# Graph network on one core: three edits in the edge pass, the relation sums and the last layer

## The chip, the cores and the metric

The kernel runs on one core of one Trainium2 chip. The metric is the device time of one execution in microseconds (us), median of several runs. A core has five engines with queues of their own: TensorE (PE; matrix products, its weight loads shown as PEld), VectorE (DVE), ScalarE (ACT), GpSimd (POOL), which here only gathers and scatters rows by index, and SyncE (SP), which issues plain transfers. They wait for one another through semaphores only. SBUF is the on-chip memory, PSUM the memory that TensorE writes and VectorE and ScalarE can read.

## The reference

6250 nodes with 64 features, 200,000 edges sorted by destination. Four layers, each on the layer-normed, rectified features `h`, each added to `x`:

```python
# layer 0: attention; i = src, j = dst, act = softplus
out_i = act(concat(h[i], edge_attr) @ W); out_j = act(concat(h[j], edge_attr) @ W)   # 4 heads x 64
alpha = act((concat(out_i, out_j) * att).sum(-1))            # one number per edge and head
alpha = segment_softmax(act(batch_norm(alpha)), i)
x += segment_sum(out_j * alpha, i).mean(heads) + bias
# layer 1
x += segment_sum(h[src], dst)
# layer 2, twice: h @ W[r] for 24 relations, one of them per edge
h = relu(segment_sum(hw[src, rel], dst) / deg);  x += h
# layer 3: five 64x64 products; neigh_low/high are means over the edges
low  = relu(h W_self)      + mean_agg(relu(h W_neigh) * deg**-0.5)
high = relu(h W_self_high) - mean_agg(relu(h W_neigh_high) * deg**-0.5)
ident = relu(h W_id)
a = softmax(sigmoid([low.w_low, high.w_high, ident.w_mlp]) @ W_att.T / 3)
x += 3 * (a0 * low + a1 * high + a2 * ident)
```

## The kernel before

Nodes stand in 50 blocks of 128 (49 used), edges in tiles of 128 (`P`), eight tiles (`G`) a group. The program is a chain of stages with barriers between them.

**Edge pass** (`edge_pass`, 202 groups in a loop of 101 trips, two groups a trip). It makes `out_i`, `out_j` and their products with `att` for each edge, sorts the edges by source (a counting sort) and scatters the rows to `rows_d`. For one group the queues run as follows. GpSimd gathers eight tiles of features (L785) and scatters the eight tiles of finished rows (L793) behind a wait for `rows_ready` (L791). TensorE takes the tiles in four pairs: a pair's products go to one of two PSUM tiles `z` (L873, L876) behind a wait for `z_free` (L870); between the pairs stand small products that keep a running count (L886, L890), each after a copy by ScalarE (L818, the wait is L885). At the group's end TensorE turns the next group's features (L866), ScalarE copies them (L824), and the next group's first pair needs that copy. ScalarE makes exp and ln (L828, L834) of each pair. VectorE does, pair by pair, `outs(q, p)`: two operations that finish softplus (L950 to `prod`, L954 to `rows`), a wait for both (L956), after which it gives `z` back to TensorE, two multiplications by `att` (L958, L960), a wait for both (L962) and a sum (L963). Between the pairs stand eight `ranks` (L941, each counts earlier edges of the same source within a tile), the next group's one-hots (L927 to L936), `pick` and `base` (L988, L992), `place` (L997, behind waits for the ranks), a copy of the edges' ends (L998), and at the end the heads' sum (L1001), which gives `rows_ready`. All orders are written out by hand.

**Relation sums** (`gather_sum`, two runs of 202 groups). GpSimd gathers 128 rows at a time (L1522), TensorE multiplies them with one-hots, VectorE adds the results to `acc` (L1223) and makes the next one-hots with one comparison per group (L1564), of `iota` and `dloc`, both in SBUF. GpSimd waits only for a free ring buffer and the index lists.

**Last layer.** Four stages: a norm; `channel_tables`, which per block turns `h` (L1802), multiplies it by five weights (L1812), rectifies (L1847) and scales (L1837); `dense_sum` (tag `l3s`), which multiplies the table with a 49-block matrix of edge counts, in two halves of its columns (L1437), each followed by an evacuation and transpositions (L1450 to L1469); and `channel_mix` (L1889 to L1913), VectorE on whole 3200-column tiles, then one store (L1873).

## Time and profile before

| | us |
|---|---|
| median of 3 runs | 14033.08 (14031.82 to 14033.41) |
| profiled execution | 14016.92, its span 14015.4 |
| edge pass, about 510 to 5384 | 4874 |
| softmax, attention, second layer, table, to 8690 | 3306 |
| relation sums, about 8690 to 10820 and 11098 to 13125 | 2130 and 2027 |
| last layer, 13160 to the end | 855 |
| busy in the span: PE, DVE, ACT, POOL | 7345.0, 7365.5, 3395.4, 8457.6 |

All busy shares are averages over stages in which different engines are the last. In a timeline a row gives start, duration, engine (a trailing q: the queue), line, operation, output and inputs, and in brackets the engine's idle time before it and what ended it. A group of part 5 gives busy time, mean duration, and idle time. Windows give busy us for PE, PEld, DVE, ACT and POOL in that order, then the granted share of TensorE's clock (1.00 is 2.4 GHz, 0.50 is 1.2 GHz), the DMA engines' busy share and GB/s. Durations of VectorE overlap the next start by a little, so what an operation costs is read from start to start.

### The profile page before, as it was taken

To read this page: it belongs to the slowest core of one execution; us is meant where nothing else is said; L and a number is where in the kernel's file an instruction comes from. 1 tells how busy PE (TensorE), PEld (TensorE's weight loads), DVE (VectorE), ACT (ScalarE), POOL (GpSimd) and SP (SyncE) were. 2 spreads that over 40 slices of the span, in tenths; PEclk is the share of its full clock that TensorE was granted. 3 is DMA by queue.
4 is the path that set the end of the run, shared out by engine and by line. 5 is a ranking of instruction groups with operands and counts; after the bars stand their busy time and mean duration, and the time that the engine had idled before them with its cause. 6 is when DMAs were issued, how large, how long until landed. Compare 5 with 4: busy or idle time off the path is not lost. (4 is left out here: it accounts for less than half of the span.)

```text
span 14015.4 us, 154885 instructions
## 1 busy us (share of the span) xinstructions
PE 7345.0 (52%) x27414; PEld 5002.7 (36%) x27414; DVE 7365.5 (53%) x15655; ACT 3395.4 (24%) x7069; POOL 8457.6 (60%) x8196
## 2 busy tenths in 40 slices
PE   4577767776777772035551297333333533333387
PEld 4344444444444441025551033333333333333233
DVE  6688888888888884647772002222223222222301
ACT  0244444444444442036661001000000100000100
POOL 1366666666666662877777501777776477777300
PEclk9888888888888886556665698555555655555588
DMA  1344444444444448036661285111111311111065
GB/s 23 91 140 143 141 142 144 139 145 140 143 140 142 140 142 65 10 105 181 182 182 53 85 294 190 25 26 25 26 25 24 128 26 26 26 26 26 11 243 212
DMA packets 1037353, 1462.78 MB, mean 104 GB/s; under 512 B 518414, under 2 KB 733934, under 8 KB 1011937
## 3 DMA queue, kind: packets, MB, share of 16 engines
q1 hardware_dynamic: 651986, 1075.95, 24.6%
q0 software_dynamic: 284800, 382.51, 10.2%
q10 hardware_dynamic: 100368, 2.41, 0.8%
q14 instruction: 165, 1.35, 0.0%
q8 instruction: 34, 0.56, 0.0%
HBM read 946.06 MB, written 512.36 MB: 104 GB/s over the span
## 5 line engine op out<-in xcount | busy, mean ns | idle before, releaser
L1522 POOL DMA_INDIRECT l2s_got<-rel_d,l2s_idx x3232 | 3252.5, 1006 | 1899.4 <-POOLq L1519 1006.0
L1548 PE MATMUL l2s_ps<-l2s_got,l2s_oh 128*128 128x65 f32 (+1 forms) x6464 | 1473.2, 421 | 2797.5 <-PEq L1546 2790.4
L873 PE MATMUL edge_z<-edge_w,edge_feats 128*128 128x512 f32 x3232 | 2092.0, 735 | 877.7 <-PEq L870 877.7
L1548 PEld LDWEIGHTS l2s_ps<-l2s_got,l2s_oh 128*128 128x128 f32 x6464 | 1409.0, 330 | 2863.0 <-issue 2863.0
L793 POOL DMA_INDIRECT rows_d<-edge_rows,edge_place x1624 | 1657.3, 1021 | 1100.1 <-POOLq L791 661.4
L1223 DVE TENSOR_TENSOR net_acc<-net_acc,l2s_ps 128x65 f32 (+1 forms) x3232 | 720.4, 223 | 2735.8 <-DVEq L1570 1877.4
L1241 POOL DMA_INDIRECT count_d<-all_list_val,all_list_idx x1568 | 1821.0, 1161 | 503.4 <-issue 464.2
L785 POOL DMA_INDIRECT edge_gath<-h_d,edge_idx x1624 | 1652.9, 1018 | 495.0 <-issue 494.7
L1354 PE MATMUL at_ps<-at_msg,at_oh 128*128 128x128 f32 x3520 | 746.3, 399 | 879.8 <-PEq L1350 863.3
L876 PE MATMUL edge_z<-edge_products,edge_oh_dstT 128*128 x3232 | 1155.5, 445 | 0.0
L876 PEld LDWEIGHTS edge_z<-edge_products,edge_oh_dstT 128*128 128x128 f32 x3232 | 737.4, 228 | 1010.2 <-issue 1010.2
L828 ACT ACTIVATE edge_soft<-edge_z 128x1024 f32<-128x1024 f32 x808 | 827.4, 1024 | 1068.2 <-ACTq L839 1035.1
L963 DVE TENSOR_REDUCE edge_dots<-edge_prod 128x16 f32<-128x1024 f32 x808 | 986.0, 1220 | 118.1
L873 PEld LDWEIGHTS edge_z<-edge_w,edge_feats 128*128 128x128 f32 x3232 | 661.1, 226 | 1047.4 <-issue 968.0
L1354 PEld LDWEIGHTS at_ps<-at_msg,at_oh 128*128 128x128 f32 x3520 | 693.9, 302 | 932.2 <-issue 932.2
L886 PE MATMUL edge_at<-edge_upto,edge_oh_loT 128*128 128x50 f32 x3232 | 594.8, 267 | 514.8 <-PEq L885 513.7
L834 ACT ACTIVATE edge_soft<-edge_soft 128x1024 f32<-128x1024 f32 x808 | 855.5, 1059 | 29.3
L886 PEld LDWEIGHTS edge_at<-edge_upto,edge_oh_loT 128*128 128x128 f32 x3232 | 580.1, 199 | 693.5 <-issue 635.0
L241 ACT ACT_TABLE_LOAD x4 | 5.1, 1283 | 3264.9 <-ACTq L240 3264.9
L1437 PE MATMUL l1s_ps<-l1s_cnt,l_h 128*64 128x512 f32 (+1 forms) x1274 | 519.4, 571 | 526.0 <-PEq L1435 526.0
L818 ACT COPY edge_upto<-edge_nxt 128x49 f32<-128x49 f32 x1616 | 316.4, 196 | 1441.8 <-ACTq L817 1432.9
L958 DVE TENSOR_TENSOR edge_prod<-edge_prod,edge_att 128x512 f32<-128x512 f32 x808 | 559.5, 692 | 195.3 <-DVEq L956 187.4
(364 smaller groups left out, 10171.3 us busy)
## 6 DMA issues: line engine op xcount, KB each, us to landing
at_rows<-rows_d SPq DMA_DIRECT2D x444, 528.0 KB
count_d<-edge_zero SPq DMA_DIRECT2D x202, 994.0 KB
l1s_cnt<-count_d SPq DMA_DIRECT2D x49, 1600.0 KB, 6.3
l3s_cnt<-count_d SPq DMA_DIRECT2D x49, 1600.0 KB, 6.3
rel_d<-l2t_out SPq DMA_DIRECT2D x100, 768.0 KB, 3.3
l1s_cnt<-count_d SPq DMA_DIRECT2D x49, 1536.0 KB, 6.0
l3s_cnt<-count_d SPq DMA_DIRECT2D x49, 1536.0 KB, 6.0
edge_drow<-loc_d SPq DMA_DIRECT2D x203, 256.0 KB
```

The costliest lines, as they stand in the source:

```text
L785: pool.indirect_dma_start(out=gath[q][:, j * D:(j + 1) * D], out_offset=None, in_=net.h0_d, in_offset=bass.IndirectOffsetOnAxis(ap=idx[q][ ...
L793: pool.indirect_dma_start(out=net.rows_d, out_offset=bass.IndirectOffsetOnAxis(ap=place[q][:, j:j + 1], axis=0), in_=rows[q][:, j, :], in_ ...
L828: s.activation(soft, z, ACT.Exp).then_inc(exp_made, 1)
L834: s.activation(soft, soft, ACT.Ln, bias=1.0).then_inc(ready, 1)
L873: pe.matmul(z[p % 2][:, t, :], feats[q][:, j * P:(j + 1) * P], w[:, :], start=True, stop=False, skip_group_check=True)
L876: ins = pe.matmul(z[p % 2][:, t, OUTJ:WIDE], oh_dstT[q][:, j * P:(j + 1) * P], products[:, bass.ds(blocks[j], OUTJ)], start=False, stop=Tr ...
L886: ins = pe.matmul(at_hi[:, j, :], oh_loT[q][:, j * P:(j + 1) * P], upto[j % 2][:, :], start=True, stop=True)
L963: v.tensor_reduce(dots[:, tiles, :].rearrange("p t h -> p (t h)"), prod[:, :, :].rearrange("p t (h d) -> p (t h) d", d=D), AX.X, ALU.add). ...
L1241: pool.indirect_dma_start(out=cells, out_offset=bass.IndirectOffsetOnAxis(ap=net.list_idx[i][:, k:k + 1], axis=0), in_=net.list_val[i][:, ...
L1354: ins = pe.matmul(ps[q][:, j, :], oh[q][:, n, :], msg[q][:, n, :], start=k == 0, stop=k == SPAN - 1)
L1522: pool.indirect_dma_start(out=got[r][:, j, 0:cols], out_offset=None, in_=table, in_offset=bass.IndirectOffsetOnAxis(ap=idx[i][:, k:k + 1], ...
L1548: ins = pe.matmul(ps[q][:, j, 0:wide], oh[q][:, j, :], got[r][:, j, 0:wide], start=True, stop=True)
```

## The change

Three edits.

1. Edge pass, VectorE's order. Each pair now writes `rows` first, then `prod`; one rank stands between the second of these and the multiplications, one between the multiplications and the sum, which is now a function `dot(p)` of its own. In pair 2 `pick` also stands ahead of the sum; in pair 3 the copy of the ends and `place` do.
2. Relation sums. The comparison reads `iota` from a copy in PSUM, made once a run.
3. Last layer. `channel_tables`, `dense_sum` and `channel_mix` become one stage. Two blocks of the table are made first; block b+2 is made between the matmuls of block b of the first half. The mix runs in two halves of 25 blocks, the first beside the second half's matmuls, and each half is stored by itself.

The buffers of the count lists also get a scope of their own, which only changes addresses.

```diff
-            def ranks(q, half):
...
+            def rank_of(q, j):
+                return v.scalar_tensor_tensor(
+                    junk_r[:, j, :], srow[q][:, j * P:(j + 1) * P], src_g[q][:, j:j + 1],
+                    before[:, :], ALU.is_equal, ALU.mult, accum_out=rank[:, j:j + 1])
 
             def outs(q, p, scattered_before=None):
                 v.wait_ge(soft_ready, 1).then_inc(soft_ready, -1)
+                if scattered_before is not None:
+                    v.wait_ge(scattered[q], scattered_before)
+                v.scalar_tensor_tensor(rows[q][:, tiles, 0:OUTJ], ..., ALU.min, ALU.max)
                 v.wait_ge(dotted, 1).then_inc(dotted, -1)
                 v.scalar_tensor_tensor(prod[:, :, 0:OUTJ], ..., ALU.min, ALU.max).then_inc(out_made, 1)
-                if scattered_before is not None:
-                    v.wait_ge(scattered[q], scattered_before)
-                v.scalar_tensor_tensor(rows[q][:, tiles, 0:OUTJ], ...).then_inc(out_made, 1)
-                v.wait_ge(out_made, 2).then_inc(out_made, -2)
+                rank_of(q, 2 * p)
+                v.wait_ge(out_made, 1).then_inc(out_made, -1)
                 v.sem_inc(z_free, 1)
                 v.tensor_tensor(prod[:, :, 0:OUTJ], ..., ALU.mult)
                 v.tensor_tensor(prod[:, :, OUTJ:WIDE], ..., ALU.mult).then_inc(multiplied, 1)
-                v.wait_ge(multiplied, 2).then_inc(multiplied, -2)
+                last = rank_of(q, 2 * p + 1)
+                if p == HALF - 1:
+                    last.then_inc(ranked, 1)
+            def dot(p):
+                v.wait_ge(multiplied, 1).then_inc(multiplied, -1)
                 v.tensor_reduce(dots[:, tiles, :]..., ALU.add).then_inc(dotted, 1)
...
                     outs(q, 2)
                     v.wait_ge(at_ready, 1).then_inc(at_ready, -1)
                     v.tensor_tensor(pick[:, :, :], ..., ALU.mult).then_inc(picked, 1)
+                    dot(2)
                     v.wait_ge(picked, 1).then_inc(picked, -1)
                     v.sem_inc(at_free, 1)
                     v.tensor_reduce(base[:, :], pick[:, :, :], AX.X, ALU.add).then_inc(based, 1)
-                    ranks(q, 1).then_inc(ranked, 1)
+                    outs(q, 3)
+                    v.tensor_copy(rows[q][:, :, OUTJ + HEADS:OUTJ + HEADS + 2], net.ends[:, bass.ds(w0, G), :])
+                    v.wait_ge(based, 1).then_inc(based, -1)
                     v.wait_ge(ranked, 1).then_inc(ranked, -1)
                     v.sem_inc(ids_free, 1)
-                    v.wait_ge(based, 1).then_inc(based, -1)
                     v.tensor_tensor(place[q][:, :], rank[:, :], base[:, :], ALU.add)
-                    v.tensor_copy(rows[q][:, :, OUTJ + HEADS:OUTJ + HEADS + 2], net.ends[:, bass.ds(w0, G), :])
-                    outs(q, 3)
+                    dot(3)
...
+        iota = t.ps("iota", [P, P])
...
-                    v.tensor_tensor(oh[q][:, :, :], net.iota[:, None, :].to_broadcast([P, G, P]),
+                    v.tensor_tensor(oh[q][:, :, :], iota[:, None, :].to_broadcast([P, G, P]),
...
+def channel_layer(net, norm, acc, own, table):
...
+                for b in TWO:
+                    turn_row(b)
+                    products(b)
+                for b0, b1 in halves:
...
+                    for b in range(NBU):
+                        pe.wait_ge(loaded[n % RING], 16).then_inc(loaded[n % RING], -16)
+                        for c in range(0, cols, 512):
+                            if c == 3 * 512 and b0 == 0 and b + 2 < NB:
+                                turn_row(b + 2)
+                            ins = pe.matmul(ps[:, c:min(c + 512, cols)], table[:, b, :], ...)
...
+                        if b0 == 0 and b + 2 < NB:
+                            products(b + 2)
...
+                tables()
+                v.wait_ge(mix_loaded, 64)
+                for b0, b1 in halves:
+                    sums(b0, b1)
+                    mix(b0, b1)
```

VectorE's queue before, at the start of a group of the edge pass (`edge_prod` and `edge_rows` are the softplus outputs, `edge_junk_r` marks a rank):

```order
L950 SCALAR_TENSOR_TENSOR edge_prod<-edge_soft,edge_z 128x2x256
L953 REGISTER_ALU x2
L954 SCALAR_TENSOR_TENSOR edge_rows<-edge_soft,edge_z 128x2x256
L958 TENSOR_TENSOR edge_prod<-edge_prod,edge_att 128x2x256
L960 TENSOR_TENSOR edge_prod<-edge_rows,edge_att 128x2x256
L963 TENSOR_REDUCE edge_dots<-edge_prod 128x16
L941 SCALAR_TENSOR_TENSOR edge_junk_r,edge_rank<-edge_srow,edge_src_g,edge_before 128x128 x4
```

The same place now:

```order
L948 REGISTER_ALU x2
L949 SCALAR_TENSOR_TENSOR edge_rows<-edge_soft,edge_z 128x2x256
L952 SCALAR_TENSOR_TENSOR edge_prod<-edge_soft,edge_z 128x2x256
L940 SCALAR_TENSOR_TENSOR edge_junk_r,edge_rank<-edge_srow,edge_src_g,edge_before 128x128
L957 TENSOR_TENSOR edge_prod<-edge_prod,edge_att 128x2x256
L959 TENSOR_TENSOR edge_prod<-edge_rows,edge_att 128x2x256
L940 SCALAR_TENSOR_TENSOR edge_junk_r,edge_rank<-edge_srow,edge_src_g,edge_before 128x128
L968 TENSOR_REDUCE edge_dots<-edge_prod 128x16
```

The ranks, four in a row before, stand singly ahead of the multiplications and of the sum; the register instructions for the scatter's wait stand ahead of the first output.

TensorE's queue before, at the end of the tables and the start of the count sum (`ch_tp` holds a turned block, `l3s_ps` the sum):

```order
L1802 MATMUL ch_tp<-all_ident,ch_hs 65x128
L1812 MATMUL ch_ps<-ch_ws,ch_ht 128x320
L118 REGISTER_ALU
L118 COMPARE_AND_BRANCH
L1789 UNCONDITIONAL_BRANCH
L1429 UNCONDITIONAL_BRANCH
L1437 MATMUL l3s_ps<-l3s_cnt,l3t_table 128x512 x6
L1437 MATMUL l3s_ps<-l3s_cnt,l3t_table 128x128
```

The same work now:

```order
L1855 MATMUL ch_tp<-ch_ws,ch_ht 128x320
L1870 MATMUL ch_ps<-ch_cnt,net_table 128x512 x3
L1851 MATMUL ch_tp<-all_ident,net_h 64x128
L1870 MATMUL ch_ps<-ch_cnt,net_table 128x512 x3
L1870 MATMUL ch_ps<-ch_cnt,net_table 128x128
L1855 MATMUL ch_tp<-ch_ws,ch_ht 128x320
```

Between the seven count matmuls of a block now stands the transposition, and behind them the product, of a later block; the two branches, which mark a change of stage, are gone.

## Rows read from the trace of the kernel before

**Rows 1.** Windows of two stretches: length, busy us (x instructions), PEclk, DMA share.
```profile
510.00:5384.00 4874.00, 3471.70 (x12120) 2113.13 (x12120) 4312.15 (x9292) 2273.34 (x4341) 3286.75 (x3224) 0.87 0.47 141
...
13160.00:13374.00 214.00, 78.46 (x151) 32.90 (x151) 48.65 (x202) 48.58 (x75) 0.00 (x0) 0.50 0.00 0
```

**Rows 2.** Source view of line 1001: ns min/median/max, first and last start.
```profile
L1001 DVE TENSOR_TENSOR edge_rows<-edge_dots x202: 191/192/196, 542.5 to 5383.8; 128x32 f32<-128x32 f32 x101
```

**Rows 3.** VectorE's timeline in one group: start us, duration, engine, line, idle time.
```profile
3010.59 0.68 DVE L950 SCALAR_TENSOR_TENSOR edge_prod<-edge_soft,edge_z 128x512 f32<-128x512 f32 x1
...
3012.11 0.69 DVE L958 TENSOR_TENSOR edge_prod<-edge_prod,edge_att 128x512 f32<-128x512 f32 x1 [0.24 <-DVEq L956]
3012.72 0.69 DVE L960 TENSOR_TENSOR edge_prod<-edge_rows,edge_att 128x512 f32<-128x512 f32 x1
3013.55 1.22 DVE L963 TENSOR_REDUCE edge_dots<-edge_prod 128x16 f32<-128x1024 f32 x1
3014.69 0.84 DVE L988 TENSOR_TENSOR edge_pick<-edge_oh_hi,edge_at 128x400 f32<-128x400 bf16 x1
3015.77 0.57 DVE L992 TENSOR_REDUCE edge_base<-edge_pick 128x8 f32<-128x400 f32 x1 [0.24 <-DVEq L990]
...
3016.80 0.35 DVE L941 SCALAR_TENSOR_TENSOR edge_junk_r<-edge_srow,edge_src_g,edge_before 128x128 bf16<-128x128 int16 x1
...
3017.07 0.35 DVE L941 SCALAR_TENSOR_TENSOR edge_junk_r<-edge_srow,edge_src_g,edge_before 128x128 bf16<-128x128 int16 x1
...
3017.78 0.17 DVE L997 TENSOR_TENSOR edge_place<-edge_rank,edge_base 128x8 uint32<-128x8 f32 x1 [0.35 <-DVEq L996]
...
3018.30 0.69 DVE L950 SCALAR_TENSOR_TENSOR edge_prod<-edge_soft,edge_z 128x512 f32<-128x512 f32 x1
```

**Rows 4.** TensorE's timeline there: the first matmul of each pair of tiles.
```profile
3005.80 1.10 PE L873 MATMUL edge_z<-edge_w,edge_feats 128*128 128x512 f32 x2 [0.18 <-PEq L870]
...
3012.93 1.10 PE L873 MATMUL edge_z<-edge_w,edge_feats 128*128 128x512 f32 x2 [2.68 <-PEq L870]
...
3019.88 1.10 PE L873 MATMUL edge_z<-edge_w,edge_feats 128*128 128x512 f32 x2 [0.81 <-PEq L870]
...
3026.42 1.06 PE L873 MATMUL edge_z<-edge_w,edge_feats 128*128 128x512 f32 x2
```

**Rows 5.** Short windows in the same group of tiles; columns as in rows 1.
```profile
3010.70:3014.10 3.40, 1.17 (x4) 0.70 (x5) 3.01 (x5) 3.23 (x5) 2.79 (x3) 1.00 0.12 31
3014.10:3017.60 3.50, 3.46 (x9) 1.98 (x7) 3.09 (x11) 1.44 (x3) 2.58 (x4) 0.51 0.12 26
```

**Rows 6.** Timeline of GpSimd: the first scatter of a group.
```profile
3023.64 0.99 POOL L793 DMA_INDIRECT rows_d<-edge_rows,edge_place  x1 [3.17 <-POOLq L791]
```

**Rows 7.** Page, part 5, relation gathers: busy us, mean ns, idle before.
```profile
L1522 POOL DMA_INDIRECT l2s_got<-rel_d,l2s_idx x3232 | 3252.5, 1006 | 1899.4 <-POOLq L1519 1006.0
```

**Rows 8.** Timeline of a relation sum: gathers beside an addition and beside a one-hot.
```profile
10005.55 0.95 POOL L1522 DMA_INDIRECT l2s_got<-rel_d,l2s_idx  x1 [0.30 <-issue]
10005.72 0.23 DVE L1223 TENSOR_TENSOR net_acc<-net_acc,l2s_ps 128x65 f32 x1 [0.30 <-DVEq L1224]
...
10008.84 1.23 DVE L1564 TENSOR_TENSOR l2s_oh<-all_iota,all_dloc 128x1024 f32<-128x1024 f32 x1 [0.81 <-DVEq L1584]
10009.32 1.57 POOL L1522 DMA_INDIRECT l2s_got<-rel_d,l2s_idx  x1 [0.30 <-issue]
```

**Rows 9.** Timeline of the last layer, as before.
```profile
13380.94 11.34 PE L1437 MATMUL l3s_ps<-l3s_cnt,l3t_table 128*128 128x512 f32 x24 [8.52 <-PEq L1435]
...
13646.05 3.49 DVE L1460 COPY l3s_turn<-l3s_ps 128x3200 f32<-128x3200 f32 x1 [272.21 <-DVEq L1459]
...
13917.92 3.36 DVE L1460 COPY l3s_turn<-l3s_ps 128x3072 f32<-128x3072 f32 x1 [254.95 <-DVEq L1459]
...
13939.25 3.49 DVE L1889 TENSOR_TENSOR mix_tmp<-net_acc,net_rdeg 128x3200 f32<-128x3200 f32 x1 [5.84 <-DMA mix_w<-in_W_att]
...
14006.13 0.40 SPq L1873 DMA_DIRECT2D out<-net_x  x1
```

More of the change, by code:

```diff
@@ L1774, in _ @@
                 done(v.tensor_tensor(net.x[:, :, :], net.x[:, :, :], h[:, 0:NB, :], ALU.add))
[L1777 removed]
+def channel_layer(net, norm, acc, own, table):
     nc, a = net.nc, net.a
+    RING = 3
+    halves = ((0, 25), (25, NB))
+    used = lambda b1: min(b1, NBU)
+    most = 25 * P
+    wide = 2 * D
     with Mem(nc, "ch") as t:
         ws = t.sb("ws", [D + 1, 5 * D])
[L1781 to L1782 removed]
         ht = [t.sb(f"ht{q}", [D + 1, P]) for q in TWO]
[L1784 to L1788 removed]
+        cnt = [t.sb(f"cnt{r}", [P, most]) for r in range(RING)]
+        wa = t.sb("wa", [P, 3, D])
+        w3 = t.sb("w3", [P, 3, 3])
+        lg = t.sb("lg", [P, 25, 3])
+        at = t.sb("at", [P, 25, 3])
+        pr = t.sb("pr", [P, 25, 3])
+        mx = t.sb("mx", [P, 25])
+        turn = norm.sq[:, :, :].rearrange("p b d -> p (b d)")
+        tmp = norm.blocks[:, 0:25, :]
+        ps = t.ps("ps", [P, most])
+        tp = t.ps("tp", [P, 512])
+        product, row = tp[:, 0:5 * D], tp[0:D, 512 - P:512]
+        some = 512 // wide
+        target = by_block(acc)
+        count_rows = net.count_d[0:NU * LD].rearrange("(b p c) -> b p c", p=P, c=LD)
+        sem = lambda name: net.sem("ch_" + name)
+        loaded = [sem(f"loaded{r}") for r in range(RING)]
+        cnt_free, summed, moved, turned, taken = (sem(x) for x in ("cnt_free", "summed", "moved", "turned", "taken"))
+        weights_loaded, mix_loaded, row_turned, copied, done, kept, scaled = (
+            sem(x) for x in ("weights_loaded", "mix_loaded", "row_turned", "copied", "done", "kept", "scaled"))
+        logits, squashed, shifted, raised = (sem(x) for x in ("logits", "squashed", "shifted", "raised"))
+        mixed, stored = sem("mixed"), sem("stored")
         with nc.Block() as block:
@@ L1805, in _, with turn_row @@
-                pe.wait_ge(weights_loaded, 160)
-                turn(0)
-                with Loop(nc, pe, NB // 2):
-                    for q in TWO:
-                        pe.wait_ge(copied, 1).then_inc(copied, -1)
-                        turn(1 - q)
-                        pe.wait_ge(scaled, 1).then_inc(scaled, -1)
-                        pe.matmul(ps[q][:, :], ht[q][:, :], ws[:, :], start=True, stop=True).then_inc(done, 1)
+                def turn_row(b):
+                    if b:
+                        pe.wait_ge(scaled, 1).then_inc(scaled, -1)
+                    pe.transpose(row, norm.blocks[:, b, :], net.ident[:, :]).then_inc(row_turned, 1)
@@ new lines, in products @@
+                def products(b):
+                    pe.wait_ge(copied, 1).then_inc(copied, -1)
+                    pe.matmul(product, ht[b % 2][:, :], ws[:, :], start=True, stop=True).then_inc(done, 1)
+                pe.wait_ge(weights_loaded, 160)
+                for b in TWO:
+                    turn_row(b)
+                    products(b)
+                n = 0
+                for b0, b1 in halves:
+                    blocks = used(b1) - b0
+                    cols = blocks * P
+                    for b in range(NBU):
+                        pe.wait_ge(loaded[n % RING], 16).then_inc(loaded[n % RING], -16)
+                        for c in range(0, cols, 512):
+                            if c == 3 * 512 and b0 == 0 and b + 2 < NB:
+                                turn_row(b + 2)
+                            ins = pe.matmul(ps[:, c:min(c + 512, cols)], table[:, b, :],
+                                            cnt[n % RING][:, c:min(c + 512, cols)], start=b == 0, stop=b == NBU - 1)
+                        if b < NBU - 1:
+                            ins.then_inc(cnt_free, 1)
+                        else:
+                            ins.then_inc(summed, 1)
+                        if b0 == 0 and b + 2 < NB:
+                            products(b + 2)
+                        n += 1
+                    if b0 == 0:
+                        pe.wait_ge(scaled, 1).then_inc(scaled, -1)
+                    pe.wait_ge(moved, 1).then_inc(moved, -1)
+                    pe.sem_inc(cnt_free, 1)
+                    for i, k0 in enumerate(range(0, blocks, some)):
+                        if i:
+                            pe.wait_ge(taken, 1).then_inc(taken, -1)
+                        for k in range(k0, min(k0 + some, blocks)):
+                            ins = pe.transpose(tp[:, (k - k0) * wide:(k - k0 + 1) * wide],
+                                               turn[:, k * P:(k + 1) * P], net.ident[:, :])
+                        ins.then_inc(turned, 1)
+                    pe.wait_ge(taken, 1).then_inc(taken, -1)
@@ new lines, in _ @@
+            @block.scalar
+            def _(s):
+                for b in range(NB):
+                    s.wait_ge(done, 1).then_inc(done, -1)
+                    s.activation(own[:, b, :], product[:, 0:3 * D], ACT.Relu).then_inc(kept, 1)
+                for _ in halves:
+                    s.wait_ge(logits, 1).then_inc(logits, -1)
+                    s.activation(lg[:, :, :], lg[:, :, :], ACT.Sigmoid).then_inc(squashed, 1)
+                    s.wait_ge(shifted, 1).then_inc(shifted, -1)
+                    s.activation(at[:, :, :], at[:, :, :], ACT.Exp).then_inc(raised, 1)
@@ new lines, in sums @@
+                def sums(b0, b1):
+                    blocks = used(b1) - b0
+                    cols = blocks * P
+                    v.wait_ge(summed, 1).then_inc(summed, -1)
+                    v.tensor_copy(turn[:, 0:cols], ps[:, 0:cols]).then_inc(moved, 1)
+                    for k0 in range(0, blocks, some):
+                        k1 = min(k0 + some, blocks)
+                        v.wait_ge(turned, 1).then_inc(turned, -1)
+                        got = tp[:, 0:(k1 - k0) * wide].rearrange("p (k w) -> p k w", w=wide)
+                        own_done(v.tensor_copy(target[:, b0 + k0:b0 + k1, 0:wide], got))
+                        v.sem_inc(taken, 1)
```

189 lines of the change are left out of this document (71 added, 118 removed).

## The prediction, made before the change was run

> **What bounds the kernel now.** I read the windows first, since the stages have different limits. The edge pass is 4874 us of the 14015, with VectorE busy 88% of it (4312 us) and TensorE's granted clock at 0.87 [rows 1]. Line 1001 comes once a group, from 542.5 to 5383.8 in 202 rows, so a group takes 4841.3/201 = 24.09 us [rows 2]. The reader should then look at VectorE's timeline in one group [rows 3]: the only idle it shows stands behind its own semaphores (0.24, 0.24, 0.35 us), never behind ScalarE or TensorE. So VectorE's own program is the group. TensorE waits 2.68 and 0.81 us ahead of pairs [rows 4], GpSimd 3.17 us for finished rows [rows 6]. In the relation sums the idle in front of a gather is 0.30 us, its pitch from issue [rows 8], with VectorE's additions far apart: GpSimd is the bound there. In the last layer the stages follow one another with nothing beside them [rows 1, 9].
>
> **The change, edge pass.** All pitches are from start to start [rows 3]. Multiplication to multiplication is 0.61, rank to rank 0.27.
>
> (a) Two outputs and their wait take 12.11 - 10.59 = 1.52; with 0.61 for the first, the second output to the multiplication is 0.91. A rank put there would let the multiplication start at 0.61 + 0.27 = 0.88, inside the wait. The rank is free: 4 x 0.27 = 1.08 us a group.
> (b) Second multiplication to sum is 0.83. With a rank it is 0.61 + 0.27 = 0.88, so 0.83 + 0.27 - 0.88 = 0.22, four times 0.88 us.
> (c) `pick` to `base` is 1.08 with its 0.24 of waiting. Behind `pick` now comes the sum, at about 0.84 - 0.08 = 0.76, and `base` follows the sum at the usual 1.14: 0.32 us.
> (d) Last rank to `place` is 0.71, with 0.35 idle. The copy of the ends now lies in it. `place` and that copy take 0.52 together, so its half, 0.26, goes; one wait is also satisfied earlier. Bounds 0.26 and 0.45; I take 0.35.
> (e) The register instructions for the scatter's wait stand ahead of the first output, behind the short L1001. No row prices them. Bounds 0 (hidden) and +0.35 (the longest idle that short instructions leave); I take +0.12.
>
> Sum: 1.08 + 0.88 + 0.32 + 0.35 - 0.12 = 2.5, so VectorE alone would do a group in 21.6 us.
>
> Then the next engines are late. GpSimd's group is the period less its wait beyond the usual 0.30: 24.09 - 2.87 = 21.2, some tenths more when its gathers no longer rest beside pair 3. TensorE: from the third pair in [rows 4] (pair 3 at 3005.80) to the next group's first 7.13; to its second 6.95, less 0.81 of waiting for VectorE, 6.14; to its third 6.54; the rest of the period 24.09 - 20.62 = 3.47, less 0.18, 3.29. Together 23.1 us as clocked here, more than 21.6. But a granted share of 0.87 means that 2 x 0.13 = 0.26 of the period, 6.3 us, ran at 1.2 instead of 2.4 GHz; at the upper level throughout the cycle would be about 23.1 - 3.1 = 20.0. The clock fell to 0.51 behind a stretch in which TensorE was busy 1.17 of 3.4 us, the wait before the next group's first pair, and that stretch ran at 1.00 [rows 5]. That wait mostly stays (it hangs on ScalarE's copy of the features, not on VectorE); the 0.81 goes. So I expect the second low stretch of a group to come less often, not always to vanish. VectorE's pace leaves TensorE 1.6 us of low-clock loss, half of today's.
>
> Three engines with 21.6, 21.2 to 21.6 and 20.0 to 23.1 do not give 21.6. I add 0.4: 22.0 us, a gain of 2.09 x 202 = 422 us. Bounds: 21.5 (-523) and 23.0 (-220).
>
> The added order of waits costs nothing else as I read it. The scatter's wait now holds back both outputs and so `z_free`, but the eight scatters it asks for start right behind their group's rows [rows 6] and last 8 x 21.2/16 = 10.6, with a full period to go. `ids_free` comes after pair 3, some 3 us later than before; SyncE's row loads that it releases are needed two pairs into the next group but one use later, over 7 us on. `at_free` comes behind `pick` and the sum's issue, still before TensorE has finished the next first pair.
>
> **Relation sums.** A gather beside an addition (SBUF and PSUM in) takes 0.95 us; one that overlaps the one-hot (both inputs in SBUF, 1.23 us) takes 1.57 [rows 8]. The mean of all 3232 is 1.006 [rows 7], so the stretching is 3232 x (1.006 - 0.950) = 181 us, all on GpSimd's chain, which is the bound. With `iota` in PSUM the one-hot has one SBUF input, like the addition. I take all 181; bounds 0 and 181. VectorE may take longer for it without cost, as it idles 0.81 us before a one-hot and more between groups. The two copies of `iota` cost under 1 us.
>
> The Trainium skill, "SBUF — State Buffer", section "Who interferes with whom", says that an instruction with at most one SBUF input does not contend with GpSimd, one with two does against GpSimd's reads. By that rule all 181 go, as in the sum. The same section also says that its own probe saw copies hold up descriptor making and `tensor_tensor` not; by that sentence the 181 have another cause and stay. The rows show a `tensor_tensor` beside the stretched gather, so the trace agrees with the first.
>
> **Last layer.** Tables took 214 us [rows 1], and the first count matmul started at 13380.94, 220.9 after 13160. Now it needs the weights, two blocks (each about 214/50 = 4.3) and the first counts: 14 us. Saved 207. In exchange TensorE does 48 transpositions and products among the counts. A block of counts is (13646.05 - 13380.94)/49 = 5.41 us for 6.25 times 512 columns [rows 9], so 0.87 per 512; a product of 320 is 0.54, a transposition of 128 at most 0.22. 48 x 0.76 = 36 us (bounds 30 and 84, the latter at the lower clock). ScalarE and VectorE get half a block, 2.7 us, for each answer, enough. The second half from 13646.05 to 13917.92 stays. From 13917.92 to the mix is 21.3 us with 5.84 idle behind weight loads and the barrier [rows 9]: that idle goes, 5. The mix with the store's issue is 14006.13 - 13939.25 = 66.9; its first half now lies beside the second half's matmuls. Sixteen operations of 3.6 become 1.9 and the short ones shrink little: 38, so 29 saved. The store's 9.3 us to the span's end falls to about 6: 3. Waits behind VectorE's own copies add 2. Sum: 207 - 36 + 5 + 29 + 3 - 2 = 206. Bounds 158 and 215.
>
> **The sum.** 422 + 181 + 206 = 809. The profiled execution of 14016.92 becomes 13208. The median of the runs is 16 us above it, 14033.08; so 13224.
>
> **Rivals.**
> R1, VectorE's full gain: TensorE's clock stays up and the period is 21.5 to 21.6: 13224 - 95 = 13129. For it: less waiting in TensorE. Against: the wait of [rows 5] has another cause.
> R2, TensorE becomes the bound with today's low stretches, 23.0 to 23.1 a group: 202 x 1.05 more, 13436. For it: [rows 4] add up to just that. Against: part of that low clock came from waits that go.
> R3, the PSUM copy doesn't free GpSimd (the stretch comes from VectorE's writes or from any long instruction): 13224 + 181 = 13405. The addition in [rows 8] is only 0.23 us long, so it proves little.
> R4, VectorE's own waits can't be filled: the instruction behind a rank then starts late by the same 0.3, as if each had to drain first. The edge pass keeps 24.09 and the time is 13646. Against it: ranks follow one another at 0.27 with a duration of 0.35. The Trainium skill, "VectorE: DVE Perf Modes", section "The DRAIN you can't avoid", has this: the flush comes after every operation and a semaphore costs nothing extra. The trace disagrees, 0.91 with a wait against 0.61 without [rows 3].
> R5, slower than before: a low clock that feeds itself in the edge pass. TensorE's cycle is 20.0 plus half of its time at the lower level. The other two edits give 387, so it decides from a period of 24.09 + 387/202 = 26.0, that is 12 us of low clock in a group, a granted share of 0.77. At 0.70, the mean of the whole span, the period is 20.0/(1 - 0.3) = 28.6 and the time 14033 - 387 + 911 = 14557. For it: the clock falls after waits, and a slower TensorE makes VectorE wait. Against: TensorE then is the one that never waits.
>
> **How the numbers follow.** Forecast 0.52, R1 0.17, R2 0.14, R3 0.11, R4 0.03, R5 0.02, and 0.01 for no change. The likeliest is 13224. The range runs from R1 to R2: 13110 to 13440. 0.2% (28 us) is about what a measurement of this kernel tells from no change; all cases but R5 and that 0.01 are faster by more: 0.97, 0.01, 0.02.
>
> **What the next profile would show.** L1008 (now the heads' sum) every 22 us; the multiplication 0.91 behind the second output with a rank between; GpSimd's wait ahead of the first scatter near 0.5 to 1.0; the granted clock of the edge pass at 0.87 or above. Gathers of the relation sums with a mean of 0.95 and none near 1.6. The first count matmul 14 us after the norm, first half near 302 us, and about 60 us from the last matmul to the end. I am wrong if the relation gathers still have a mean of 1.0, or the edge pass is over 23.2 or under 21.3 us a group.

## The result, and the profile after

The changed kernel takes 13121.02 us (median of 4 runs, 13117.08 to 13136.03); the kernel before takes 14032.45 (4 runs, 13999.49 to 14033.41). The ratio is 0.936, with an interval of 0.934 to 0.937: 911 us faster. The forecast was 13224 (808 less), its range 13110 to 13440, so the result lies 11 us above the lower end. In the profiled executions the span falls by 896.0, from 14015.4 to 13119.4:

```
part of the program (us)                      before     after    change   forecast
start to the first heads' sum                  542.5     522.1     -20.4        0
edge pass, first to last heads' sum           4841.3    4357.4    -483.9     -422
from there to the relation gathers            3309.7    3306.5      -3.1        0
relation gathers, first to last               4417.3    4240.0    -177.3     -181
last gather to the end                         904.7     693.4    -211.3     -206
```

The 20.4 are no work of the change: most of them, 16 us, are the node products ahead of the loop, code that nobody touched, whose 98 matmuls took 25.2 us at a granted clock of 1.00 in the profile of after and 40.5 us at 0.53 in that of before.

The heads' sum, first its row in the view of one line, then the edge pass in the windows (columns as in rows 1):

```profile
L1008 DVE TENSOR_TENSOR edge_rows<-edge_dots x202: 191/192/194, 522.1 to 4879.5; 128x32 f32<-128x32 f32 x101
```
```profile
522.07:4879.50 4357.43, 3225.86 (x12046) 2005.24 (x12044) 4155.12 (x9247) 2262.67 (x4317) 3367.52 (x3208) 0.89 0.52 157
```

A group takes 4357.4/201 = 21.68 us, where it took 24.09 [rows 2]. VectorE is now busy 95% of it, and the clock is 0.89 against 0.87 [rows 1]. VectorE's timeline, one pair and the tail of a group, answers to [rows 3]:

```profile
3001.06 0.75 DVE L936 TENSOR_SCALAR edge_oh_loT<-edge_lrow,all_part 128x1024 f32<-128x1024 bf16 x1
3001.72 0.68 DVE L949 SCALAR_TENSOR_TENSOR edge_rows<-edge_soft,edge_z 128x512 f32<-128x512 f32 x1
3002.32 0.69 DVE L952 SCALAR_TENSOR_TENSOR edge_prod<-edge_soft,edge_z 128x512 f32<-128x512 f32 x1
3002.92 0.35 DVE L940 SCALAR_TENSOR_TENSOR edge_junk_r<-edge_srow,edge_src_g,edge_before 128x128 bf16<-128x128 int16 x1
3003.20 0.08 DVE L940 DVE_READ_ACCUMULATOR edge_junk_r<-edge_srow,edge_src_g,edge_before 128x1 f32 x1
3003.25 0.69 DVE L957 TENSOR_TENSOR edge_prod<-edge_prod,edge_att 128x512 f32<-128x512 f32 x1
3003.86 0.68 DVE L959 TENSOR_TENSOR edge_prod<-edge_rows,edge_att 128x512 f32<-128x512 f32 x1
3004.46 0.34 DVE L940 SCALAR_TENSOR_TENSOR edge_junk_r<-edge_srow,edge_src_g,edge_before 128x128 bf16<-128x128 int16 x1
...
3004.73 0.88 DVE L994 TENSOR_TENSOR edge_pick<-edge_oh_hi,edge_at 128x400 f32<-128x400 bf16 x1
3005.51 1.22 DVE L968 TENSOR_REDUCE edge_dots<-edge_prod 128x16 f32<-128x1024 f32 x1
...
3010.11 0.17 DVE L1001 COPY edge_rows<-edge_ends 128x16 f32 x1
3010.44 0.17 DVE L1005 TENSOR_TENSOR edge_place<-edge_rank,edge_base 128x8 uint32<-128x8 f32 x1 [0.15 <-DVEq L1003]
3010.59 1.22 DVE L968 TENSOR_REDUCE edge_dots<-edge_prod 128x16 f32<-128x1024 f32 x1
3011.92 0.19 DVE L1008 TENSOR_TENSOR edge_rows<-edge_dots 128x32 f32<-128x32 f32 x1
3012.73 0.69 DVE L949 SCALAR_TENSOR_TENSOR edge_rows<-edge_soft,edge_z 128x512 f32<-128x512 f32 x1 [0.62 <-DVEq L946]
```

Second output to multiplication is 0.93 with a rank inside, as it was 0.91 without one. The idle of [rows 3] is gone but for 0.15 at `place`. The 0.62 ahead of the next group's first output is no wait for another engine, though the view puts it down to L946: this group ends a trip of the loop, and branch and register instructions make it 0.81 from the heads' sum to that output, where it is 0.31 in the group that doesn't end one (before 0.69 and 0.27). GpSimd in the same stretch, and both of its lines and the relation gathers on the page (busy us, mean ns, idle before):

```profile
3001.33 1.31 POOL L793 DMA_INDIRECT rows_d<-edge_rows,edge_place  x1 [0.30 <-issue]
3002.95 0.96 POOL L793 DMA_INDIRECT rows_d<-edge_rows,edge_place  x1 [0.30 <-issue]
3004.21 1.16 POOL L793 DMA_INDIRECT rows_d<-edge_rows,edge_place  x1 [0.30 <-issue]
3005.68 0.96 POOL L793 DMA_INDIRECT rows_d<-edge_rows,edge_place  x1 [0.30 <-issue]
```
```profile
L793 POOL DMA_INDIRECT rows_d<-edge_rows,edge_place x1624 | 1766.5, 1088 | 515.0 <-issue 495.3
L785 POOL DMA_INDIRECT edge_gath<-h_d,edge_idx x1624 | 1640.9, 1010 | 494.9 <-issue 457.1
L1530 POOL DMA_INDIRECT l2s_got<-rel_d,l2s_idx x3232 | 3073.8, 951 | 1901.8 <-POOLq L1527 1024.3
```

The wait of [rows 6] (3.17) has gone: nothing but the 0.30 of issue stands between two issues. A group is 8 x (1.088 + 1.010) + 16 x 0.307 = 21.7, the whole period. GpSimd is the engine that never rests now, with issues stretched to 1.31 and 1.16. Its scatters started 1.0 us behind the heads' sum in the kernel before; now they fall back to between 4 and 8 us behind it and stay there. How that reaches the others is seen twelve times in the pass (28 us of VectorE's time): TensorE's transposition has to wait for gathered rows, and VectorE for the first output of the next group.

```profile
3153.37 0.63 PE L866 MATMUL edge_tp<-all_ident,edge_gath 128*128 128x128 f32 x4 [1.87 <-DMA edge_gath<-h_d,edge_idx]
...
3165.61 0.69 DVE L949 SCALAR_TENSOR_TENSOR edge_rows<-edge_soft,edge_z 128x512 f32<-128x512 f32 x1 [2.94 <-DVEq L946]
```

The relation gathers have a mean of 0.951, where it was 1.006 [rows 7]. The last layer, TensorE's first rows and VectorE's first copy of the second half, which answer to [rows 9]:

```profile
12480.80 0.39 PE L1851 MATMUL ch_tp<-all_ident,net_h 128*64 128x128 f32 x1 [45.62 <-DMA ch_ws<-in_b_neigh_high]
...
12487.73 4.33 PE L1870 MATMUL ch_ps<-ch_cnt,net_table 128*128 128x512 f32 x6
```
```profile
13058.20 3.36 DVE L1921 COPY net_sq<-ch_ps 128x3072 f32<-128x3072 f32 x1 [218.58 <-DVEq L1920]
```

First counts 7 us behind the first transposition, the first half until 12784 (296.5, before 265.1), the copy of the second half 61.2 us ahead of the end.

### The profile page after: what moved, and what is told of

Its sections match the earlier page's. It is cut to its first block and busy times, and to the rows that moved or that the text cites. A ratio compares the mean times of both kernels' runs of the same rounds, so it can differ in the third digit from the quotient of the medians.

```text
span 13119.4 us, 153826 instructions
## 1 busy us (share of the span) xinstructions
PE 7068.2 (54%) x27413; PEld 4885.6 (37%) x27413; DVE 7217.2 (55%) x15584; ACT 3368.0 (26%) x7048; POOL 8372.3 (64%) x8196
## 5 line engine op out<-in xcount | busy, mean ns | idle before, releaser
L1530 POOL DMA_INDIRECT l2s_got<-rel_d,l2s_idx x3232 | 3073.8, 951 | 1901.8 <-POOLq L1527 1024.3
L873 PE MATMUL edge_z<-edge_w,edge_feats 128*128 128x512 f32 x3232 | 1966.7, 694 | 584.9 <-PEq L870 583.7
L1248 POOL DMA_INDIRECT count_d<-counts_list_val,counts_list_idx x1568 | 1816.2, 1158 | 503.4 <-issue 464.2
L793 POOL DMA_INDIRECT rows_d<-edge_rows,edge_place x1624 | 1766.5, 1088 | 515.0 <-issue 495.3
L876 PE MATMUL edge_z<-edge_products,edge_oh_dstT 128*128 x3232 | 1095.1, 424 | 0.0
L876 PEld LDWEIGHTS edge_z<-edge_products,edge_oh_dstT 128*128 128x128 f32 x3232 | 698.7, 216 | 937.2 <-issue 937.2
L968 DVE TENSOR_REDUCE edge_dots<-edge_prod 128x16 f32<-128x1024 f32 x808 | 981.8, 1215 | 0.0
L873 PEld LDWEIGHTS edge_z<-edge_w,edge_feats 128*128 128x128 f32 x3232 | 632.1, 217 | 707.4 <-issue 639.7
L1572 DVE TENSOR_TENSOR l2s_oh<-l2s_iota,all_dloc 128x1024 f32<-128x1024 f32 x404 | 494.6, 1225 | 300.9 <-DVEq L1593 161.5
L1305 ACT ACTIVATE at_far<-all_iota,at_loc 128x128 f32<-128x128 f32 x1768 | 540.9, 388 | 423.8 <-ACTq L1303 423.8
```

Source lines behind the costliest of these rows:

```text
L793: pool.indirect_dma_start(out=net.rows_d, out_offset=bass.IndirectOffsetOnAxis(ap=place[q][:, j:j + 1], axis=0), in_=rows[q][:, j, :], in_ ...
L873: pe.matmul(z[p % 2][:, t, :], feats[q][:, j * P:(j + 1) * P], w[:, :], start=True, stop=False, skip_group_check=True)
L876: ins = pe.matmul(z[p % 2][:, t, OUTJ:WIDE], oh_dstT[q][:, j * P:(j + 1) * P], products[:, bass.ds(blocks[j], OUTJ)], start=False, stop=Tr ...
L968: v.tensor_reduce(dots[:, tiles, :].rearrange("p t h -> p (t h)"), prod[:, :, :].rearrange("p t (h d) -> p (t h) d", d=D), AX.X, ALU.add). ...
L1248: pool.indirect_dma_start(out=cells, out_offset=bass.IndirectOffsetOnAxis(ap=net.list_idx[i][:, k:k + 1], axis=0), in_=net.list_val[i][:, ...
L1530: pool.indirect_dma_start(out=got[r][:, j, 0:cols], out_offset=None, in_=table, in_offset=bass.IndirectOffsetOnAxis(ap=idx[i][:, k:k + 1], ...
```

## The experiments

All twelve ran beside the kernel before. Three, of one run each, shared a chip on which it takes 14020 us. On the other chips (nine runs) it took 17261 to 17635: there, as I read it, engines inside loops get their instructions late. The profile shows idle time for which it knows no wait; what makes it is open. VectorE's additions in the relation sums of the run iota_only, usually 0.52 apart, with "issue" ahead of them:

```profile
12511.62 0.22 DVE L1223 TENSOR_TENSOR net_acc<-net_acc,l2s_ps 128x65 f32 x1 [3.28 <-issue]
12515.17 0.22 DVE L1223 TENSOR_TENSOR net_acc<-net_acc,l2s_ps 128x65 f32 x1 [3.32 <-issue]
...
12517.83 0.22 DVE L1223 TENSOR_TENSOR net_acc<-net_acc,l2s_ps 128x65 f32 x1 [0.30 <-DVEq L1224]
```

Durations of instructions are the same there, periods of loops are not. So from those nine I read durations and local pitches, and the last layer, which as changed has no loop (in its form before the tables have one: 914 to 917 us there, 905 in the kernel before above); only what is said below of their times is about the time.

**One edit each.** The kernel before with the edge pass's diff alone, the relation sums' alone, the last layer's alone.

> The kernel before with the new order of the edge pass alone. If the three edits are independent, the edge pass has the period that it has with all three, 21.68 us: 201 x (24.09 - 21.68) = 484 us less than before, about 13548 us, and gathers of the relation sums keep their mean of 1.006 us. The rival: part of the 484 belongs to the other edits (code elsewhere, addresses of buffers), and less than 440 us go here.

> The kernel before with the PSUM copy of iota alone. If the one-hot's second SBUF input is what stretches the gathers, their mean falls from 1.006 to 0.95 us, none is near 1.6, and 3232 x 0.055 = 177 us go: about 13855 us. The rival R3 (the stretch comes from the one-hot's writes or its length, and another edit shortened the gathers): the mean stays at 1.0 and the time within 30 us of before.

> The kernel before with the one-stage last layer alone. If the edits are independent, 205 to 211 us go, about 13825 us, nearly all of it ahead of the first count matmul. The rival: what the stage gains depends on what stands before it (clock, transfers still under way), and less than 180 us go.

Measured against 17265.56: 17816.88 (ratio 1.032, 1.030 to 1.035), 17362.49 (1.006, 1.003 to 1.009), 17016.59 (0.985, 0.981 to 0.988). The last layer takes 694.9 us from the last gather, against 914.3 and 916.5 in the two others: 220 saved, whatever stands around it. The gathers of the relation sums, pages of iota_only and last_only:

```profile
L1523 POOL DMA_INDIRECT l2s_got<-rel_d,l2s_idx x3232 | 3073.4, 951 | 2756.2 <-POOLq L1520 1756.8
```
```profile
L1522 POOL DMA_INDIRECT l2s_got<-rel_d,l2s_idx x3232 | 3225.4, 998 | 2513.1 <-POOLq L1519 1525.6
```

The edit alone takes the mean to 951 and R3 falls. But here GpSimd waits more ahead of the gathers (1757 us of idle, not 1526): from first to last they take 5093 us, not 5003, and the whole is 97 us slower. What the shorter gathers are worth is shown by the kernels before and after alone. The new order makes the edge pass slower here: 34.87 us a group in edge_only, 32.14 and 32.10 in the two with the old order, 201 x 2.75 = 553 us more. (The median of edge_only is 551 longer; its profiled execution, from which the 34.87 come, was its fastest and 435 longer, so the rest of the program was shorter in it.) Which wait of the new order costs this where instructions come late I did not find out. The three expected times (13548, 13855, 13825) rest on a kernel before of 14033 and cannot be compared here; the additivity that I expected is neither shown nor refuted.

**What stretches an issue.** Behind the one-hots of three groups in four the run doses adds VectorE work whose output nobody uses, two operations each (put here in short form):

```diff
+ for _ in TWO:                     # behind the one-hot of group r
+     r == 0: tensor_tensor(x32, net.iota (SBUF), net.dloc)     L1607
+     r == 1: tensor_tensor(x16, in16[0], in16[1])  (bfloat16)  L1611
+     r == 2: tensor_scalar(x32, in16[0], net.part)             L1614
```

> All three edits, and extra VectorE work with no use for the output in the relation sums, to see what stretches a GpSimd gather (0.95 us otherwise): in the first of every four groups two one-hots with both inputs in SBUF (float32, as before the change), in the second two comparisons of two bfloat16 SBUF tiles, in the third two comparisons of one bfloat16 SBUF tile with a column of SBUF, in the fourth nothing. Theory (two SBUF inputs are what counts): gathers beside the float32 pair take 1.3 us or more, those beside the one-input comparison 0.95, and bfloat16 with two inputs stretches too, as line 932 seems to in the edge pass. Rival (length or writes count): all three stretch alike. Rival (only 4-byte data count): the bfloat16 pair leaves 0.95.

Three gathers that start inside such an instruction, each with it (x2 is two in a row):

```profile
12066.90 2.59 DVE L1607 TENSOR_TENSOR l2s_x<-all_iota,all_dloc 128x1024 f32<-128x1024 f32 x2
...
12223.30 0.75 DVE L1614 TENSOR_SCALAR l2s_x<-l2s_in,all_part 128x1024 f32<-128x1024 bf16 x1 [0.16 <-issue]
...
12358.98 1.52 DVE L1611 TENSOR_TENSOR l2s_x<-l2s_in 128x1024 bf16<-128x1024 bf16 x2
```
```profile
12067.01 1.93 POOL L1533 DMA_INDIRECT l2s_got<-rel_d,l2s_idx  x1 [0.30 <-issue]
...
12223.56 1.31 POOL L1533 DMA_INDIRECT l2s_got<-rel_d,l2s_idx  x1 [0.30 <-issue]
...
12359.28 1.19 POOL L1533 DMA_INDIRECT l2s_got<-rel_d,l2s_idx  x1 [0.30 <-issue]
```

All three kinds stretch a gather, and the one-hot with iota in PSUM, as long as the first, none. So length is not it; nor, against my theory, is a second SBUF tile needed: L1614 reads one, and a column. The bfloat16 pair has two such cases only, but the changed edge pass has more: 92 issues start in L932, a one-hot of two bfloat16 tiles in SBUF, and every one takes 348 to 368 ns more than 951; they are held beyond its end into L934, of the same kind. And it is not overlap, but the start that counts. A gather that starts inside the instruction is held until 0.12 us before its end: in the kernel before, 312 gathers start over 0.05 us into the one-hot with over 0.2 us of it left; they have 689 ns of it left on average and take 563 more than 951 (difference 126, spread 3). Counted the same way, L936 gives 475 and 354 in the changed edge pass, L957 450 and 336, L959 398 and 284, and the ranks in the run odd_in_blocks, with an int16 tile and a mask in SBUF, 286 and 158. One that started first is not touched (300 cases beside the one-hot before, 0 ns more), and neither are the 14 that start within 0.042 us of the one-hot's own start. The reductions (L968, 709 starts, +15 ns) and the outputs from PSUM (L949, +1) hold nothing.

**The multiplications' weights in PSUM.**

```diff
+ att_ps = e.ps("att_ps", [P, 2, OUTJ])       # copied once from att
- ... att[:, 0:1, :] ... att[:, 1:2, :]
+ ... att_ps[:, 0:1, :] ... att_ps[:, 1:2, :]
```

> All three edits, and the two multiplications of a pair read the attention weights from a copy in PSUM, so that they have one SBUF input, as the one-hot of the relation sums now has. Theory: in the changed edge pass GpSimd is the bound, 16 issues of 1.355 us are its 21.68, and the stretched part of them (0.952 without company) comes from these multiplications: the mean of its gathers and scatters falls from 1.05 towards 0.97, the period to VectorE's 21.0 to 21.2, and 100 to 135 us go: 12985 to 13020 us. Rival 1: VectorE is the bound and its 0.85 us of waiting comes from TensorE's low clock: issues get shorter, the period stays at 21.6 to 21.7 and the time within 25 us of 13121. Rival 2: the multiplications are not what stretches the issues: their mean stays at 1.05 and nothing changes. If the kernel before runs far above 14033 us (in four runs on one chip it took 17266, with engines that got their instructions late), the period says nothing on this and only the mean of the issues counts.

> The kernel of the run att_psum again, on a chip where engines get their instructions in time (before at 14020 to 14033 us), if it is one. Of the 16 issues that a group asks of GpSimd, 1.06 us a group were stretched beside the two multiplications in the changed kernel. Theory (GpSimd's issues are its bound, at 21.68 us a group, and VectorE alone needs 20.99): the mean of the issues falls from 1.05 to 0.99 or below, the period to 21.0 to 21.2, and 100 to 135 us go from 13121: 12985 to 13020 us. Rival (TensorE's low clock holds VectorE up for those 0.69 us): the issues get shorter, the period stays within 0.15 of 21.68.

Both fell on a chip with late instructions: 17838.55 (1.033, 1.030 to 1.036) and 17956.56 (1.018, 1.015 to 1.020). The issues in the edge pass, pages of edge_only (same order, weights in SBUF) and att_psum:

```profile
L793 POOL DMA_INDIRECT rows_d<-edge_rows,edge_place x1624 | 1716.6, 1057 | 3262.7 <-POOLq L791 2811.9
L785 POOL DMA_INDIRECT edge_gath<-h_d,edge_idx x1624 | 1597.4, 984 | 500.9 <-issue 494.5
```
```profile
L794 POOL DMA_INDIRECT rows_d<-edge_rows,edge_place x1624 | 1613.6, 994 | 3537.9 <-POOLq L792 3087.2
L786 POOL DMA_INDIRECT edge_gath<-h_d,edge_idx x1624 | 1605.5, 989 | 501.1 <-issue 494.7
```

The scatters fall from 1057 to 994. Issues that start inside a multiplication: 427 in edge_only with 112 us above 951 ns, 416 in att_psum with 4. So the copy in PSUM frees GpSimd from the multiplications, and rival 2 falls. What it is worth where GpSimd is the bound no run shows. The 100 to 135 us of my expectations are too much by VectorE's pitches: their 20.99 us leaves out the loop's end, and from 21.68 to its 21.24 (point 1 of the next section) there are only 88 us in the whole pass.

**The same with fillers for TensorE**, ahead of the wait for the features.

```diff
+ pe.wait_ge(z_free, 1).then_inc(z_free, -1)          # was in outs, for p = 0
+ for _ in range(10): pe.matmul(z[0][:, 0, 0:P], net.ident, net.ident, ...)
```

> The kernel of the run att_psum (attention weights read from PSUM in the edge pass), and in addition ten matmuls of 128 columns without use while TensorE waits for the next group's features. Where engines get their instructions as in the first runs of before and after: the issues beside VectorE's multiplications are free, so a group is VectorE's own 20.99 us if TensorE's low clock cost nothing, or stays 0.3 to 0.6 above it if the clock was part of the changed kernel's 21.68 and the fillers do not keep it up; the theory (GpSimd's issues are the bound) expects 21.0 to 21.2, near 13000 us, with a granted clock above 0.95 in the edge pass. Where instructions come late (before at over 17000 us) the period says nothing; then only the issues (mean below 1.00 us) and the granted clock are read.

> As att_psum_again, and ten matmuls of 128 columns without use while TensorE waits for the next group's features. If what is left of waiting with the weights in PSUM is TensorE's low clock behind that wait, the fillers keep the clock up (above 0.95 granted in the edge pass) and the period falls by up to the rest above 20.99; if GpSimd was all of it, the period is that of att_psum_again within 0.05 us and the clock alone changes. Should the fillers end later than the features are ready, TensorE starts its first pair late, which VectorE feels only if TensorE's cycle of 20.0 us at full clock plus them is over 21.

18003.60 (one run, before 17276.50) and 18195.74 (1.032, 1.030 to 1.035): late instructions again, 36.5 and 37.5 us a group. Whether a higher clock would gain time where they come in time stays open.

**Ranks back in blocks**, in all_in_blocks all eight, in odd_in_blocks 1, 3, 5 and 7 only (shown):

```diff
- last = rank_of(q, 2 * p + 1)                        # in outs
+ for j in (1, 3): rank_of(q, j)                      # behind dot(0)
+ for j in (5, 7): rank_of(q, j)                      # behind base
```

> All three edits, but the eight ranks stand again in two blocks of four (behind the first sum and behind base), so that only the exchanged outputs, the sum ahead of base and the copy ahead of place are left of the new order. My terms (a) 1.08 and (b) 0.88 us a group are undone: VectorE alone needs 21.0 + 1.96 = 23.0 us, is the bound again, and the period is 23.0 to 23.1: 201 x 1.35 = 271 us more than with all edits, about 13392 us. If GpSimd's 21.68 and not VectorE is the bound to a larger part than I think, or the ranks were never free in the waits, the period rises by less than 0.9 us and the time is below 13300.

> All three edits, but the four odd ranks stand in two blocks of two again, so that only the even ones (in the wait between the second output and the first multiplication) are spread. Read from VectorE's starts, which hold whatever bounds the group: second output to multiplication stays at 0.92 with the even rank in it (term a: 0.27 saved four times), second multiplication to sum is 0.83 again instead of 0.87 with a rank (term b: 0.23 lost each time). Rival R4 (a wait cannot be filled): the sum starts 0.83 behind the multiplication with the rank or without, plus 0.27.

all_in_blocks fell on a chip with late instructions, 17866.93 (1.033, 1.031 to 1.036), so its period says nothing. VectorE's pitches without waits (worked out as in point 1 of the next section, without the loop's end) add up to 22.65 us in it, 1.66 over the changed kernel's 20.99; my terms (a) and (b) say 1.96. odd_in_blocks ran on the undisturbed chip: 13243.27 (one run), edge pass 4457.4/201 = 22.18 us, 0.50 over the changed kernel (the two other runs on that chip, which leave the edge pass as changed, have 21.69 and 21.70). Its VectorE at a pair of two kinds:

```profile
3005.32 0.68 DVE L959 TENSOR_TENSOR edge_prod<-edge_rows,edge_att 128x512 f32<-128x512 f32 x1
3006.14 1.22 DVE L965 TENSOR_REDUCE edge_dots<-edge_prod 128x16 f32<-128x1024 f32 x1
...
3016.32 0.68 DVE L959 TENSOR_TENSOR edge_prod<-edge_rows,edge_att 128x512 f32<-128x512 f32 x1
3016.92 0.87 DVE L993 TENSOR_TENSOR edge_pick<-edge_oh_hi,edge_at 128x400 f32<-128x400 bf16 x1
3017.70 1.21 DVE L965 TENSOR_REDUCE edge_dots<-edge_prod 128x16 f32<-128x1024 f32 x1
```

Without a rank the sum follows at 0.82, with one at 0.87: the wait can be filled, R4 falls. But in the third pair `pick` already fills it, and in the fourth the copy of the ends: a rank there saves nothing more. In every second group VectorE waits here for ScalarE's ln ahead of the first output (0.94 behind the heads' sum, not 0.31; 62 us in the pass), and GpSimd waits 0.5 ahead of the scatters in nearly every group, so neither is the bound of this kernel. A loop through TensorE and ScalarE is what is left; I did not take it apart.

**The last layer's two halves of the gain.** The first edit is tables_first, the second mix_at_end.

```diff
- for b in TWO:  turn_row(b); products(b)             # the other 48 among the counts
+ for b in range(NB):  turn_row(b); products(b)
```
```diff
- for b0, b1 in halves:  sums(b0, b1); mix(b0, b1)
+ for b0, b1 in halves:  sums(b0, b1)
+ for b0, b1 in halves:  mix(b0, b1)
```

> All three edits, but in the last layer all 50 blocks are transposed and multiplied ahead of the first count matmul, instead of 2 ahead and 48 among the counts. My term 'saved 207' says that the tables' chain (4.8 us a block: transposition, copy, product, scaling) is what went, not the barriers between stages: the first count matmul starts 48 x 4.3 to 4.8 = 206 to 228 us later after the first transposition, the first half shrinks by the 31 us that the mixed-in products took, and the time from the last gather to the end grows by 175 to 200 us from the changed kernel's 693 to 701. Rival (the gain came from the joined stage, its early loads and missing barriers): it grows by less than 60.

> All three edits, but both halves of the last layer are mixed after the second half's sums. My term 29 says that the first half's mix lies hidden beside the second half's matmuls: without it 38 us of mixing come behind the last matmul again and the store of the first half with them; the time from the last gather to the end grows by 38 to 45 us. Rival (the mix of the first half slows the second half's matmuls or its evacuation by as much as it hides): within 10 us of the changed kernel.

Same undisturbed chip, one run each: 13268.45 and 13166.18. From the end of the last gather to the end of the program 826.3 and 730.2, in odd_in_blocks, with the layer as changed, 692.6: +133.7 and +37.6. The first is below the 175 to 200 that I expected, and far above the rival's 60. TensorE of tables_first at two blocks:

```profile
12502.47 0.40 PE L1851 MATMUL ch_tp<-all_ident,net_h 128*64 128x128 f32 x1 [1.10 <-PEq L1850]
12503.44 1.40 PE L1855 MATMUL ch_tp<-ch_ws,ch_ht 65*128 65x320 f32 x2 [0.58 <-PEq L1854]
12505.95 0.40 PE L1851 MATMUL ch_tp<-all_ident,net_h 128*64 128x128 f32 x1 [1.10 <-PEq L1850]
```

A block takes 3.48 us, not the 4.8 that I had read from the first two: 48 x 3.48 = 167, less the 31 that the products no longer take among the counts, is 136. So of the saved stretch 167 was the chain; some 40 are the shorter chain per block (214/50 = 4.3 before) and the missing stage border. The mix is 38, as its term said.

## Why the prediction was right

1. **Edge pass, VectorE's program.** Pitches from start to start, taken where nothing else is waited for (the 15th percentile at each place, 201 groups), add up to 23.81 before and 20.99 after. These are groups that don't end a trip of the loop; the others need 0.42 and 0.50 more behind the heads' sum, so on average it is 24.03 and 21.24: 2.79 saved, forecast 2.5. (a) 0.92 + 0.27 - 0.92 = 0.27, four times 1.09 (1.08). (b) 0.83 + 0.27 - 0.87 = 0.23, four times 0.92 (0.88). (c) 1.09 becomes 0.78 less 0.01: 0.33 (0.32). (d) last rank to the next instruction 1.22 becomes 0.74: 0.48, my bound was 0.45 and my value 0.35. (e) 0.31 instead of 0.27 behind the heads' sum, and 0.81 instead of 0.69 where a trip ends: 0.04 and 0.12 (0.12). The sum holds; the split between (b), (c) and (d) does not, since either of two instructions fills the wait of pairs three and four.
2. **The allowance of 0.4.** I had 21.6 for VectorE where it is 21.24. The engine that never waits is GpSimd. I had 21.2 and "some tenths more"; it is 21.68. More of its issues start inside a multiplication, 819 of 3248 with 214 us, before 607 with 111; over all instructions the excess above 951 ns is 319 us, before 221. The allowance had no mechanism of its own, and its amount was about right by luck: 0.44 for 0.4. Of these 0.44 (88 us in the pass) 28 us are the twelve stalls behind GpSimd's gathers; 42 more are short waits for ScalarE's ln, so the loop through TensorE and ScalarE is nearly as long, and how far the period would fall without GpSimd's limit is open. The 21.68 for 22.0 are 62 of the 87 us by which the span fell further than forecast, 20 more lying ahead of the loop. R1's time came out (13129), but not by R1: the clock is 0.89, and VectorE still waits 0.44 us a group.
3. **TensorE (R2, R5).** The clock rose from 0.87 to 0.89, TensorE's waits ahead of L873 fell from 878 to 585 us, and GpSimd has no wait left that TensorE could cause. In a group the wait of [rows 4] ahead of the first pair stays (2.9), as the prediction had it.
4. **Relation sums.** 177 us of 181. The rule of the Trainium skill ("SBUF — State Buffer", "Who interferes with whom") that I took, by the count of SBUF inputs, agrees with the one-hot (951 ns with one, 563 ns more with two). L936 and L1614 hold GpSimd with one SBUF tile. That is no exception to the rule: for one input the section leaves out the two-port modes, in which VectorE takes the pair of ports that GpSimd shares, and names `tensor_scalar` among the operations that can enter one. The rows agree in so far as 1024 elements take 0.75 us there and 1.22 in the reduction; no run here tells the modes apart. Its other sentence, that its own probe saw `tensor_tensor` not hold up descriptor making, does not agree with the 563 ns here, and there the measurement decides.
5. **Last layer.** 211 for 206. First half +31.4 (36; 0.65 us for a pair of transposition and product), the tail 97.5 to 61.2 (36.3; my 5 + 29 + 3 - 2 = 35).
6. **What no step had.** 20 us ahead of the loop, which are luck: in odd_in_blocks, with the same code there, the first heads' sum comes at 541.7 again. And above all the chip: the gain of the edge pass holds where instructions come in time. Elsewhere the new edge order cost 3.2%.

## What to carry to other kernels

Add up an engine's own pitches without its waits, the loop's end with them, for every engine, before giving a change its full gain: the period is the largest of these sums or more, and speeding one engine changes the others' sums. Where GpSimd issues indirect DMAs back to back, look at which VectorE instruction runs when an issue starts; an operand in PSUM took the hold away twice. A gap that a view puts down to a semaphore can be the loop's own branch and register instructions: compare the groups that end a trip with those that don't. Time a tuned loop on more than one chip.

## What was not expected of the hardware

- An issue on GpSimd that starts inside certain VectorE instructions is held to 0.12 us before their end (up to 2.00 us instead of 0.95); one that starts before is free. Operations with two tiles in SBUF, of float32, bfloat16 or int16, and `tensor_scalar` on a bfloat16 tile (1024 in 0.75 us) do it; reductions (1024 in 1.22 us) and operations with one of two tiles in PSUM don't. So a shorter VectorE program can lengthen GpSimd's: 319 us of excess, before 221.
- The same program took 13999 to 14033 us on some chips and 17261 to 17635 on others, with equal durations of instructions and idle time of 3.3 us put down to "issue" between short ones. One and the same chip gave 17266 and 17635 at two times, and none was seen at both levels; the cause is open.
- A stage that nobody changed (node products) took 16 us more or less by the clock that it met.
